# One transformer block on one core: routed experts without sorting, 14 equal chunks, attention by halves

## What is computed

```python
x = x + tanh(g_xattn) * attention(k=ctx, v=ctx, q=layernorm(x))     # one head, block by block
h = layernorm(x)
shared = (silu(h @ w1) * (h @ w2)) @ w3                             # hidden width 512
scores = sigmoid(h @ router_w)                                      # 16 experts
top2   = top_k(scores + expert_bias, 2)                             # gates: the scores of the two
routed = sum over the two of gate * (silu(h @ r1[e]) * (h @ r2[e])) @ r3[e]   # hidden width 128
x = x + tanh(g_ffn) * (shared + routed)
```

## Time and profile before

| | us |
|---|---|
| median of 2 timed runs | 96.69 |
| lowest and highest | 96.5, 96.88 |
| span of the profiled execution | 112.6 |

### The profile page before, as it was taken

One profiled execution on the slowest core, in us unless ns is written; L12 is line 12 of the kernel. 1 busy time (PEld: TensorE's weight loads), 2 busy tenths in 40 slices (PEclk: granted clock), 3 DMA queues, 4 the chain that ended last, 5 costly groups with the idle time before them and its releaser, 6 DMA issues.

```text
span 112.6 us, 1632 instructions
## 1 busy us (share of the span) xinstructions
PE 81.5 (72%) x437; PEld 65.4 (58%) x437; DVE 41.3 (37%) x180; ACT 37.7 (33%) x102; POOL 48.7 (43%) x63
## 2 busy tenths in 40 slices
PE   4889999979999999970022999149694629399910
PEld 4768749959996556640012998139593529245900
DVE  0096008883823483000204335132272134122680
ACT  1326239682809742001003334013352123006700
POOL 4049960054000677777730036627357645730200
PEclk9999999997559999999555559976999975559998
DMA  2992009999993018453684658867741153212406
GB/s 42 286 333 113 0 4 265 147 144 174 158 148 48 23 45 255 129 128 129 128 223 88 184 170 214 262 184 210 199 160 50 47 174 89 60 41 73 122 10 177
DMA packets 19311, 15.31 MB, mean 136 GB/s; under 512 B 1424, under 2 KB 18448, under 8 KB 19296
## 3 DMA queue, kind: packets, MB, share of 16 engines
q1 hardware_dynamic: 16208, 11.57, 46.9%
q0 software_dynamic: 1184, 2.44, 6.3%
q10 hardware_dynamic: 1904, 1.14, 4.5%
HBM read 9.14 MB, written 6.00 MB: 134 GB/s over the span
## 4 chain that ended last, share of the span: by engine, by line
PE 54%; another core or an unknown queue 13%; issue 13%; DMA 5%; DVE 5%; ACT 4%; ACTq 2%; DVEq 0%
PE bank L1054 7%; PE bank L1062 7%; PE bank L1055 6%; DMA ctx_sb<-in_ctx_dram 5%; PE bank L863 5%; PE bank L878 4%; PE bank L1012 3%; PE bank L1021 3%; PE bank L1043 3%; PE bank L902 3%; PE bank L1013 3%; PE bank L963 2%; DVE hid L738 2%; PE bank L908 2%
## 5 line engine op out<-in xcount | busy, mean ns | idle before, releaser
L472 POOL DMA_INDIRECT placed_y<-tile_y,tile_place x21 | 20.1, 957 | 23.1 <-DVE tile_place L806 13.5
L461 POOL DMA_INDIRECT sorted_x<-x2n,slot x16 | 15.5, 972 | 14.7 <-DMA sorted_x<-tile_x 10.1
L1054 PE MATMUL bank<-tile_xT,tile_w 128*128 128x128 f32 x44 | 11.3, 347 | 7.4 <-issue 4.8
L1062 PE MATMUL bank<-tile_w,tile_hid 128*128 128x128 f32 x44 | 10.3, 328 | 7.0 <-issue 3.8
L1054 PEld LDWEIGHTS bank<-tile_xT,tile_w 128*128 128x128 f32 x44 | 8.7, 246 | 8.6 <-issue 8.6
L573 ACT ACTIVATE silu_t<-bank 128x512 f32<-128x512 f32 x8 | 4.8, 597 | 26.0 <-remote 15.4
L606 ACT ACTIVATE tile_silu<-bank 128x128 f32<-128x128 f32 x22 | 6.1, 277 | 19.8 <-PE bank L1055 10.8
L1062 PEld LDWEIGHTS bank<-tile_w,tile_hid 128*128 128x128 f32 x44 | 8.0, 230 | 8.0 <-issue 8.0
L813 DVE TENSOR_TENSOR tile_hid<-tile_silu,bank 128x128 f32<-128x128 f32 x22 | 6.3, 286 | 17.2 <-ACT tile_silu L606 10.0
L1043 PE MATMUL bank<-ident,tile_x 128*128 128x128 f32 x24 | 6.2, 351 | 8.3 <-issue 8.3
L738 DVE TENSOR_TENSOR hid<-silu_t,bank 128x512 f32<-128x512 f32 x8 | 5.5, 686 | 17.3 <-issue 11.1
(11 more groups left out here) (132 smaller groups left out, 121.6 us busy)
## 6 DMA issues: line engine op xcount, KB each, us to landing
tile_w<-in_routed_w_dram SPq DMA_DIRECT2D x22, 192.0 KB, 2.4
sorted_x<-tile_x SPq DMA_DIRECT2D x1, 2967.0 KB, 21.2
tile_x<-sorted_x SPq DMA_DIRECT2D x8, 129.0 KB, 2.3
shared_sb<-in_shared_w_dram SPq DMA_DIRECT2D x1, 768.0 KB, 7.6
tile_x<-sorted_x ACTq DMA_DIRECT2D x4, 129.0 KB
x_sb<-in_x_dram SPq DMA_DIRECT2D x2, 256.0 KB, 4.9
picked_y<-placed_y SPq DMA_DIRECT2D x2, 256.0 KB, 3.3
picked_y<-placed_y SPq DMA_DIRECT2D x4, 128.0 KB, 2.4
```

The lines of the kernel that those rows point to most:

```text
L461: pool.indirect_dma_start(sorted_x[:, :], bass.IndirectOffsetOnAxis(slot[:, k * B + b:k * B + b + 1], 0), x2n[:, k, b, :], None).then_inc( ...
L472: pool.indirect_dma_start(placed_y[:, :], bass.IndirectOffsetOnAxis(tile_place[:, j:j + 1], 0), tile_y[:, j, :], None).then_inc(y_placed[j ...
L1054: nc.tensor.matmul(dst[:, 0:P], tile_w[:, j % WEIGHT_RING, 0:P], xt, start=True, stop=True)
L1062: nc.tensor.matmul(bank[j % 2][:, 0:D], tile_hid[:, j % 3, :], tile_w[:, j % WEIGHT_RING, 2 * P:3 * P], start=True, stop=True)\
```

## The change

The sorting, all indirect transfers and the tables in DRAM are gone. The routed experts are computed on whole blocks in place:

- TensorE sums the one-hot choices over the tokens (`count`). DVE finds the two experts used most (`find_dense`). They are computed for all 8 blocks: four items `("dense", k, half)`.
- The remaining pairs of block and expert that are used at all are numbered. The eight highest of them are *places*; each is one block of 128 tokens through one expert. Two items `("tiles", g)` of four places each take their block, expert and gate column from registers. Empty places point at a block of zeroes.
- If more than 8 pairs are left, a branch (`total > PLACES`) runs all 16 experts over both halves one after the other, with gates only for the pairs that have no place.
- A token's gate for an expert it did not choose is zero, so `acc` receives gate times result (`add_item`).

Each item has the size of a shared chunk: two products of 512 columns (or eight of 128), one silu, one product and four down products. So there are 14 equal chunks: 8 shared, 4 dense, 2 of places. `hid` has a ring of 3.

The attention runs by halves. For the first half the turned x is used as it is: Wq is centred (`wq_centred`), the score's bias is a product of its own (`score_bias`), and DVE multiplies the scores by the row's inverse deviation while it adds that bias (`scaled`). For the second half POOL scales x by the inverse deviation before the turn. The row sum of the probabilities comes from a column of ones in `vo`. The second half's probabilities, attention, residual, second norm and router lie between the shared chunks. Sigmoid is computed as 0.5 tanh(x/2) + 0.5. The second norm is written out in full and turned once, for the router too. At the start seven bf16 products of 512 columns without use run on TensorE, and pairs of them stand at two later places.

On TensorE the order from the first shared chunk is: share_up(0), turn_probs(2), turn_probs(3), share_up(1), attend(2), attend(3), share_down(0), share_up(2), router(0), share_down(1), share_up(3), turn of the second half, share_down(2), share_up(4), share_down(3), share_up(5), router(1), share_down(4), count(0), share_up(6), share_down(5), share_up(7), share_down(6), count(1), and then what the core of the diff shows. On DVE it is: share(0), add_attention(2), share(1), add_attention(3), x2_moments(2), x2_moments(3), share(2), four normalise, share(3), pick(0), share(4), add_base(0), choose(0), share(5), share(6), pick(1), choose(1), share(7), find_dense.

```diff
+    PLACES = 8
+    GROUP = 4
+    PAIRS = B * E
+    FIRST = E - 1
+    SHARED = 2 * HJ
+    ITEMS = [("tiles", 0), ("dense", 0, 0), ("tiles", 1), ("dense", 1, 0), ("dense", 0, 1), ("dense", 1, 1)]
+    COUNT = SHARED + len(ITEMS)
+    HID_RING = 3
...
+            sp.wait_ge(dense_ready, 1)
+            for k in range(TOP):
+                e = sp.value_load(dense_index[0:1, k:k + 1], min_val=0, max_val=E - 1)
+                sp.dma_start(dense_w[:, k, :], routed(e)).then_inc(dense_loaded[k], 16)
+            sp.wait_ge(places_ready, 3)
+            for j in range(PLACES):
+                e = sp.value_load(place_expert[0:1, j:j + 1], min_val=0, max_val=E - 1)
+                sp.dma_start(place_w[:, j, :], routed(e)).then_inc(place_loaded[j], 16)
+            sp.wait_ge(total_ready, 1)
+            total = sp.value_load(left_total[0:1, 0:1], min_val=0, max_val=PAIRS)
+            with sp.If(total > PLACES):
...
+            def find_dense():
+                dve.wait_ge(counts_done, 2)
+                step(nc.vector.reduce_sum(expert_use[:, :], COUNTS[:, 0:PAIRS].rearrange("p (b e) -> p e b", e=E), AX))
+                step(nc.vector.max(most_used[:, :], expert_use[:, :]))
+                nc.vector.max_index(dense_index[:, :], most_used[:, :], expert_use[:, :]).then_inc(dense_ready, 1)
+                step(nc.vector.scalar_tensor_tensor(used_number[:, :], COUNTS[:, 0:PAIRS], 0.0, pair_number[:, :], ALU.is_gt, ALU.mult))
+                dve.wait_ge(dense_ready, 1)
+                step(nc.vector.tensor_scalar(not_first[:, :], expert_index[:, :], dense_index[:, 0:1], None, ALU.not_equal))
+                step(nc.vector.scalar_tensor_tensor(not_dense[:, :], expert_index[:, :], dense_index[:, 1:2], not_first[:, :],
+                                                    ALU.not_equal, ALU.mult))
+            def find_places():
+                step(nc.vector.tensor_tensor(left_number[:, :].rearrange("p (b e) -> p b e", e=E),
+                                             used_number[:, :].rearrange("p (b e) -> p b e", e=E),
+                                             not_dense[:, None, :].to_broadcast([P, B, E]), ALU.mult))
+                step(nc.vector.max(place_number[:, :], left_number[:, :]))
+                nc.vector.tensor_scalar(place_column[:, :], place_number[:, :], float(FIRST), None, ALU.add).then_inc(places_ready, 1)
+                nc.vector.tensor_scalar(is_left[:, :], left_number[:, :], 0.0, None, ALU.is_gt).then_inc(places_ready, 1)
+                dve.wait_ge(places_ready, 1)
+                step(nc.vector.tensor_scalar(place_expert[:, :], place_column[:, :], E - 1, None, ALU.bitwise_and))
+                nc.vector.tensor_scalar(place_block[:, :], place_column[:, :], 4, None, ALU.arith_shift_right).then_inc(places_ready, 1)
+            def finish_places():
+                dve.wait_ge(places_ready, 3)
+                step(nc.vector.reduce_sum(left_count[:, :], is_left[:, :], AX))
+                nc.vector.tensor_copy(left_total[:, :], left_count[:, :]).then_inc(total_ready, 1)
+                dve.wait_ge(slots_ready, 3)
+                step(nc.vector.tensor_tensor(left_gates[:, FIRST + 1:], gates[:, :, :].rearrange("p b e -> p (b e)"), is_left[:, :], ALU.mult))
...
+            find_dense()
+            find_places()
+            finish_places()
+            add_base(1)
+            dense = nc.values_load_multi_w_load_instructions(dense_index[0:1, 0:TOP], engines=[ENGINE.DVE], min_val=0, max_val=E - 1)[1]
+            columns = nc.values_load_multi_w_load_instructions(place_column[0:1, :], engines=[ENGINE.DVE], min_val=FIRST, max_val=FIRST + PAIRS)[1]
+            blocks = nc.values_load_multi_w_load_instructions(place_block[0:1, :], engines=[ENGINE.DVE], min_val=0, max_val=B)[1]
+            total = dve.value_load(left_total[0:1, 0:1], min_val=0, max_val=PAIRS)
+            share(SHARED)
+            dve.wait_ge(base_ready, 2)
+            with dve.If(total > PLACES):
...
+            def add_item(i):
+                item = ITEMS[i - SHARED]
+                dve.wait_ge(down_done, i + 1)
+                for q in range(GROUP):
+                    src = LAST[i % 2][:, q * D:(q + 1) * D]
+                    if item[0] == "tiles":
+                        j = GROUP * item[1] + q
+                        dve.wait_ge(added, added_before(i) + q)
+                        to = acc[:, bass.ds(blocks[j], 1), :].rearrange("p b d -> p (b d)")
+                        gate = left_gates[:, bass.ds(columns[j], 1)]
+                    else:
+                        if q == 0:
+                            dve.wait_ge(added, added_before(i))
+                        b = HALF * item[2] + q
+                        to = acc[:, 1 + b, :]
+                        gate = gates[:, b, bass.ds(dense[item[1]], 1)]
+                    nc.vector.scalar_tensor_tensor(to, src, gate, to, ALU.mult, ALU.add).then_inc(added, 1)
+            for i in range(SHARED + 1, COUNT):
+                share(i)
+                add_item(i - 1)
+            add_item(COUNT - 1)
...
+            keep_warm(7, bank[7])
...
+            share_down(6)
+            count(1)
+            pe.wait_ge(total_ready, 1)
+            total = pe.value_load(left_total[0:1, 0:1], min_val=0, max_val=PAIRS)
+            pe.wait_ge(places_ready, 3)
+            blocks = nc.values_load_multi_w_load_instructions(place_block[0:1, :], engines=[ENGINE.PE], min_val=0, max_val=B)[1]
+            pe.wait_ge(slots_ready, 3)
...
+            def item_up(i):
+                item = ITEMS[i - SHARED]
+                free_banks(i)
+                if item[0] == "tiles":
+                    for m, done in enumerate((gate_done, up_done)):
+                        for q in range(GROUP):
+                            j = GROUP * item[1] + q
+                            if m == 0:
+                                pe.wait_ge(place_loaded[j], 16)
+                            xt = x2nT[:, bass.ds(blocks[j], 1), :].rearrange("p b s -> p (b s)")
+                            last = nc.tensor.matmul(UP[i % 2][m][:, q * P:(q + 1) * P], place_w[:, j, m * P:(m + 1) * P], xt, start=True, stop=True)
+                        last.then_inc(done, 1)
                 else:
+                    pe.wait_ge(dense_loaded[item[1]], 16)
+                    for m, done in enumerate((gate_done, up_done)):
+                        nc.tensor.matmul(UP[i % 2][m][:, :], dense_w[:, item[1], m * P:(m + 1) * P], x2nT[:, slots(item[2]), :],
+                                         start=True, stop=True).then_inc(done, 1)
+            def item_down(i):
+                item = ITEMS[i - SHARED]
+                pe.wait_ge(hid_ready, i + 1)
+                if i >= SHARED + 2:
+                    pe.wait_ge(added, added_before(i - 1))
+                for q in range(GROUP):
+                    w = place_w[:, GROUP * item[1] + q, :] if item[0] == "tiles" else dense_w[:, item[1], :]
+                    last = nc.tensor.matmul(LAST[i % 2][:, q * D:(q + 1) * D], hid[:, i % HID_RING, q * P:(q + 1) * P], w[:, 2 * P:3 * P],
+                                            start=True, stop=True)
+                last.then_inc(down_done, 1)
+            item_up(SHARED)
+            share_down(7)
+            with pe.If(total > PLACES):
...
+            for i in range(SHARED + 1, COUNT):
+                item_up(i)
+                item_down(i - 1)
+            item_down(COUNT - 1)
```

More of the change, by code:

```diff
@@ L627, in _ @@
[L627 to L630 removed]
+                    src = scaled[:, b, :] if b < HALF else SCORES[p][:, (b % 2) * S:(b % 2 + 1) * S]
+                    nc.scalar.activation(probs[:, b, :], src, ACT.Exp, bias=neg_max[:, b:b + 1]).then_inc(probs_ready, 1)
+            exponentials(0)
@@ new lines, in _ @@
+            share(0)
+            add_attention(2)
+            share(1)
+            add_attention(3)
+            x2_moments(2)
+            x2_moments(3)
+            share(2)
+            for b in range(HALF, B):
+                normalise(b)
+            share(3)
+            pick(0)
+            share(4)
+            add_base(0)
+            choose(0)
+            share(5)
+            share(6)
+            pick(1)
+            choose(1)
+            share(7)
+            find_dense()
+            find_places()
@@ new lines, in _ @@
+            pe.wait_ge(gT_first_ready, 1)
+            for p in range(2):
+                if p == 1:
+                    pe.wait_ge(gT_second_ready, 1)
+                for b in (2 * p, 2 * p + 1):
+                    last = nc.tensor.matmul(SCORES[p][:, (b % 2) * S:(b % 2 + 1) * S], gT[:, b, :], ctxT[:, b, :], start=True, stop=True)
+                last.then_inc(scores_done, 1)
+            pe.wait_ge(ctx_loaded[1], 16)
+            turn(bank[4], ctx_sb, HALF, HALF).then_inc(ctx_turned, 1)
@@ new lines, in _ @@
+            pe.wait_ge(x2nT_ready, 1)
+            pe.wait_ge(x2nT_ready_too, 2)
+            pe.wait_ge(vo_ready, 2)
+            share_up(0)
```

(28 more changed lines are left out.)

1214 lines of the change are left out of this document (492 added, 722 removed).

## The result

| | before | after |
|---|---|---|
| median, us | 96.69 | 90.64 |
| lowest and highest, us | 96.5, 96.88 | 90.6, 90.68 |
| span of the profiled execution, us | 112.6 | 88.3 |

The ratio after to before is 0.937 (95% interval 0.933 to 0.942): faster, by 6.1 us.

What follows compares the result with a forecast made beforehand. It took chained waits, POOL's serial zeroing, scatters and placings, and TensorE's half clock as bounds. The new order, built up through head, shared phase, register waits, items and tail, came to 91.4, less 2.2 = 89 us; range 79 to 97.

Steps and rivals of the forecast that it cites:

- the two waits: TensorE gaps: about 10 us before the first tile item, some 5 us before item_down(8), granted clock 0.50 in both.
- What bounds the kernel now: Profile of before: 13.7 us of the 112.6 us span taken as a hold-up, leaving 98.9, 2.2 above the timed median.
- The head: Start to first shared product: 24.4 us, bounds 21.7 to 27, TensorE at half clock until 12.9.
- rows 6: Profile rows of before near the start: products at the 1.2 GHz rate, thirteen small transposes not bringing full rate by 12.8 us.
- The shared phase: Shared chunks with the second half's attention inside: 23.8 us, all on TensorE, ending at 48.2, with DVE fitting in.
- Selection, loads and registers: After the last count: fourth place lands at 58.8, down ends at 62.9, 19 DVE register loads take 8.0, reaching 70.9.
- Items and tail: After share(8) at 71.6: 12.2 us of products plus 2.5 for half clock, to 86.3; then tail, to 91.4.
- Cheap registers with full clock: Register loads cost 3 to 5 us, items run at full clock, head 2.7 shorter: 81 us; chance 0.22.
- rival 2: Clock stays half through the items: up to 9.7 us more, half of the items so gives 94; chance 0.12.
- rival 3: DVE registers between add_base(1) and share(8) at 1.2 us each: 104 us, slower from 0.93 apiece; chance 0.05.
- The branch: A ninth pair sends all through 32 serial rounds of about 5.2 us: over 250 us; chance 0.02.
- The "no change" case: Head gains only 8 us and registers stand at 16.3: 96 us; chance 0.09.

Runs made afterwards that it cites:

- Experiment 4: The kernel before, unchanged, timed and profiled a second time: 97.36 us, with a span of 94.6.
- experiment 1: Kernel after with share_down(7) moved on TensorE to right behind the last count, ahead of the place items: 85.21 us, ratio to before 0.887.
- experiment 5: Kernel after with DVE's register reads ahead of add_base(1) and 38 unused bf16 products behind the last count: 81.36 us, ratio to before 0.847.
- experiment 6: Kernel after with expert numbers written as constants, so all ten weight transfers start at the beginning: 89.06 us, ratio to before 0.923.
- experiment 2: Kernel after with DVE's register reads moved ahead of add_base(1), TensorE's order kept: 82.26 us, ratio to before 0.854.
- experiment 7: Kernel after with dense items first, share_down(7) and 15 unused products behind the last count, register reads and transfers rearranged, branch last: 75.94 us, ratio to before 0.787.
- experiment 3: Kernel after without the seven unused bf16 products at the start: 92.79 us, ratio to before 0.964.

## Why the prediction was right, and where two errors cancelled

The mechanism, the two waits and the half clock behind each came as forecast. By the steps of the prediction:

| step | forecast, us | measured, us |
|---|---|---|
| first shared product at | 24.4 (21.7 to 27) | 22.56 |
| shared phase, to the last count | 23.8 | 23.8 |
| from there to the end of share_down(7) | 14.7 | 14.3 |
| DVE's register reads | 8.0 (5.1 to 16.3) | 8.1 |
| from the end of hid(8) to TensorE's last product | 14.7 | 14.7 |
| from there to the end of the span | 5.1 | 3.9 |
| span | 91.4 | 88.3 |
| from the span to the time | -2.2 | +2.3 |

**What bounds the kernel now.** This is the step that failed. I took 13.7 us off the span for a stretch in which I took the whole core to be held up, and then -2.2 us "that still separate it from the median". Experiment 4 shows that the execution had lost 18.0 us, over all its stages, and that the time is 2.8 us above the span (2.3 in after): 112.6 - 18.0 + 2.3 = 96.9, close to before's median. The term from the span to the time was mis-sized by 4.5 us, and the sum's 3.1 us too many hid it. That the forecast came within 1.6 us is luck to that extent. Either correction alone would have given 86.1 or 93.7, both still in the range.

**The head** was 1.8 us too long against after's profile, in which the turn at 6.44 already ran at the full rate; I had counted the chain at half clock. In four of the six other profiles with the seven products it did run at half clock, to about 9 us, and there the forecast of 24.4 is the nearer (24.03 to 24.56), in part by luck, since I had let the half clock last to 12.9. The Trainium skill, "TensorE: Matmul & The Clock Gate" (The HAM clock gate), by whose rule the sum was to be 2.7 us less, is nearer in after and experiments 1 and 5 (21.7 against 22.35 to 22.64). The reading of rows 6, that thirteen transposes did not bring the full rate, also holds for one execution only: in experiment 4 the turn at 6.89 behind the same transposes took 0.66 us, the full rate, before the clock fell again. The POOL power of two columns took 0.70 us, where I used the 1.03 of four columns.

**The shared phase** was right to 0.1 us, since TensorE never stood (23.94 of 24.00 busy at full clock): the chunk's pace of before carried over, and all of DVE's 14.2 us fitted behind it.

**Selection, loads and registers.** SP's reads and issues came 1.1 us apart (1.2 forecast) and the fourth transfer landed 10.4 us behind the last count (10.6 forecast). I had left TensorE's own reads out of the sum. They ended at 54.1, hidden by the transfers, so they cost nothing here; experiment 6 shows that they would have with faster transfers. The branch that is not taken had no term either: it holds TensorE's queue for 3.93 us, in after nearly all beside products that were queued ahead (experiment 1). The total for DVE's reads, 8.0, was right for a reason that I had not given: I put it between grouped and single loads. The loads are grouped (four of them, 2.3 us together) and the arithmetic and check per register, 0.275 us with gaps, makes the greater part. The Trainium skill, "DMA: Bandwidth & Descriptors" (Latency and other measured facts), prices the load alone: by it I estimated 3 us in all. Its floor of about 600 ns agrees with three of four loads (753, 633 and 604 ns; the last took 313), and the page's price is not what decided. Two sums of this part are slightly off: the parts of SP's read make 0.54 us and not 0.57, and 58.8 + 0.43 + 1.72 + 1.8 is 62.75 and not 62.9. Neither moves the forecast by more than 0.3 us.

**Items and tail.** The half clock behind the second rest cost what I had taken: item_down(8) 2.08 instead of 1.05, item_up(10) 2.8 instead of about 1.8, the rest in gaps. The tail was 1.2 too long because the last silu and product lay beside item_down(12): they are no term of the sum.

**The rivals.** Cheap registers with full clock (81) did not happen, and experiments 2 and 5 show what it would have been worth: 82.3 and 81.4. The clock recovered both times (rival 2). A register on DVE cost 0.43 us all in, far from the 0.93 from which rival 3 decides. The branch was never taken in any run, so the price of taking it stays an estimate. The "no change" case fell with the registers, 8.1 us and not 16.3; the head came 12.7 us earlier by the profile that I had, but 9.4 by the second one, near the 8 of that rival.

**Where the gain went.** The shared phase starts 9.4 us earlier than in before's undisturbed profile and the indirect transfers are gone, yet the time fell by 6.1. The two rests of the new order, 7.8 us and 6.8 us, and their half clock took back more than half of what there was to win: with both covered and the branch put last (experiment 7) the same computation needs 75.94.

## What to carry to other kernels

When numbers from the data steer a kernel, count every register on every engine that reads it, and put the reads where the engine would wait anyway, ahead of an instruction that waits and not behind it. Give the time between the choice and its weights to work that needs neither registers nor those weights, and only then fill what is left to hold the clock. Look for the branches on each engine's queue as well: one that is never taken can hold what is queued behind it. Before a sum is built on a profile that is longer than the timed median, take a second profile: what was lost is found by comparing the two stage by stage, not by the unnamed pieces of the chain. A rate read in one profile near the start is a rate of that execution.

## What the runs showed of the hardware that was not expected

- A read of several registers is one load of 0.60 to 0.75 us and then 0.275 us per register on DVE and on TensorE alike (0.183 + 0.023, and 0.146 + 0.018, and gaps). On SP, reading one and issuing its transfer takes 1.1 us.
- DVE's four additions of a place item start 0.52 us apart in after (71.99, 72.52, 73.04), four of a dense item take 1.13 us together. By the code each addition of a place item waits for the one before (0.35 us and 0.17 of wait), those of a dense item only for the first; what the addresses from registers add was not separated.
- A branch that is not taken holds TensorE's queue for 3.4 to 4.05 us in every variant here, where the same test takes 0.07 us on DVE's queue and 0.05 on ACT's and SP's in after. Up to 1.99 us of it showed as a gap (experiment 5). Why it is so long on TensorE's queue stays open.
- The granted clock reads full at the start of after's profile and its variants, although products there run at half the rate (the turn of 1.06 us in experiment 3): near the start the pace of products tells it, not the slices.
- With the same seven products ahead, TensorE ran at the full rate from the turn at 4.65 us in one profile (experiment 5), and still at half with the product at 9.03 in another (experiment 2).
- One execution in the profiles had SP's checks at 0.70 us instead of 0.018 for a stretch, and was 18.0 us longer in all; the cause of both stays open.
